# Loops written out and the gathers of the expert stage reordered in a spiking attention plus mixture-of-experts kernel

## The reference

```python
xn = layernorm(x)
Q, K, V = (spike(layer_norm(xn @ W.T + b, g, beta) - 1.0) for W in (Wq, Wk, Wv))  # 0 or 1
attn = (Dh - hamming(Q, K)) + log_pe_bias                # 16 heads of 16, no softmax
out = spike(attn * scale @ V - 0.5)
s = spike(layer_norm(out @ Wo.T + bo, go, betao) - 1.0)
r = rms_norm(xn) * ffn_scale
ids = argmin(dist2(r, centroids))                        # one expert of eight for each row
a, g = split(r @ up_w[ids])                              # 256 -> 2 x 512
y = (a * silu(g)) @ down_w[ids]                          # 512 -> 256
return x + s * silu(y + xn)
```

## Time and profile before

| | us |
|---|---|
| median of 3 runs (378.72 to 380.95) | 378.81 |
| the profiled execution | 379.37 |
| its span, first to last instruction | 377.6 |
| PE busy | 356.3 |
| DVE busy | 305.4 |
| ACT busy | 240.7 |
| POOL busy | 232.7 |

### The profile page before, as it was taken

One profiled execution on the slowest core, in us unless ns is written; L12 is line 12 of the kernel. 1 busy time (PEld: TensorE's weight loads), 2 busy tenths in 40 slices (PEclk: granted clock), 3 DMA queues, 4 the chain that ended last, 5 costly groups with the idle time before them and its releaser, 6 DMA issues.

```text
span 377.6 us, 9198 instructions
## 1 busy us (share of the span) xinstructions
PE 356.3 (94%) x2463; PEld 300.8 (80%) x2464; DVE 305.4 (81%) x783; ACT 240.7 (64%) x646; POOL 232.7 (62%) x295
## 2 busy tenths in 40 slices
PE   7999999999999999989977999999999999999992
PEld 4778888888877888867756888888888888888881
DVE  6989999998877798988648777778888777778874
ACT  5498899888956497865425656555555556555561
POOL 4877777877621169674664666666666666666642
PEclk9999999999999999999999999999999999999999
DMA  7596667555199634364131223222223233222000
GB/s 234 178 303 175 211 194 248 194 163 159 57 175 218 196 97 126 117 195 119 51 99 51 68 58 97 80 70 87 78 83 90 74 97 89 78 90 64 28 17 0
DMA packets 31921, 45.42 MB, mean 120 GB/s; under 512 B 4161, under 2 KB 25858, under 8 KB 31764
## 3 DMA queue, kind: packets, MB, share of 16 engines
q1 hardware_dynamic: 25248, 29.73, 27.0%
q0 software_dynamic: 6416, 15.26, 14.1%
q10 hardware_dynamic: 228, 0.10, 0.1%
HBM read 36.84 MB, written 15.63 MB: 139 GB/s over the span
## 4 chain that ended last, share of the span: by engine, by line
PE 73%; DVE 9%; POOL 4%; issue 4%; DMA 4%; ACT 2%; another core or an unknown queue 2%; ACTq 0%; POOLq 0%; DVEq 0%
PE bank L705 23%; PE bank L508 16%; PE bank L724 13%; PE bank L688 4%; PE bank L622 3%; PE bank L583 3%; DMA row_a<-rows_a,slot_id 3%; PE bank L677 3%; PE bank L487 2%; PE bank L586 2%; DVE up_lo L1309 1%; PE bank L522 1%; POOL pv L1515 1%; PE bank L526 1%
## 5 line engine op out<-in xcount | busy, mean ns | idle before, releaser
L1379 DVE TENSOR_TENSOR d_lo<-down_sb,d_hi 128x1024 fp32r<-128x1024 f32 x38 | 46.6, 1225 | 29.2 <-ACT d_hi L938 28.3
L1524 POOL DMA_INDIRECT row_a<-rows_a,slot_id x39 | 40.4, 1036 | 46.7 <-DVE e_o L1361 29.7
L938 ACT ACTIVATE d_hi<-down_sb 128x1024 fp32r x38 | 40.3, 1060 | 41.9 <-PE bank L724 20.0
L1577 POOL DMA_INDIRECT out_x<-e_o,slot_id x39 | 44.4, 1139 | 19.4 <-issue 14.4
L705 PE MATMUL bank<-up_hi,e_xh 128*128 x156 | 51.9, 414 | 0.5 <-ACT e_xh L909 0.5
L1530 POOL DMA_INDIRECT row_s<-rows_s,slot_id x39 | 41.0, 1051 | 16.0 <-issue 11.6
L705 PE MATMUL bank<-up_hi,e_xl 128*128 x156 | 48.5, 392 | 1.0 <-DVE e_xl L1320 1.0
L705 PE MATMUL bank<-up_lo,e_xh 128*128 x156 | 48.4, 391 | 0.0
L909 ACT ACTIVATE e_xh<-bank 128x256 fp32r<-128x256 f32 x39 | 15.0, 384 | 44.1 <-PE bank L677 20.7
L831 ACT ACTIVATE junk<-bank 128x256 bf16<-128x256 f32 x96 | 35.4, 378 | 2.9 <-PE bank L508 2.7
L508 PE MATMUL bank<-w_hi,x_hi 128*128 128x264 f32 (+1 forms) x128 | 35.5, 359 | 0.0
(11 more groups left out here) (243 smaller groups left out, 973.6 us busy)
## 6 DMA issues: line engine op xcount, KB each, us to landing
up_raw<-in_up_w SPq DMA_DIRECT2D x16, 512.0 KB, 4.3
rows_a<-xn SPq DMA_DIRECT2D x32, 129.0 KB, 2.4
rows_a<-in_x SPq DMA_DIRECT2D x8, 512.0 KB, 12.7
xs<-in_x SPq DMA_DIRECT2D x7, 512.0 KB, 3.8
down_sb<-in_down_w SPq DMA_DIRECT2D x5, 512.0 KB, 5.9
rows_s<-s_out SPq DMA_DIRECT2D x8, 256.0 KB, 2.8
down_sb<-in_down_w SPq DMA_DIRECT2D x6, 256.0 KB, 5.8
blk_tab<-in_blocks SPq DMA_DIRECT2D x1, 1024.0 KB, 6.9
```

The lines of the kernel that those rows point to most:

```text
L938: act.activation(d_hi[:, :, :], down_sb[:, bass.ds(e, 1), :, :].rearrange("p a c n -> p (a c) n"), ACT.Copy).then_inc(d_high, 1)
L1379: V.tensor_tensor(d_lo[:, :, :], down_sb[:, bass.ds(e, 1), :, :].rearrange("p a c n -> p (a c) n"), (d_hi if k < ST else d_end)[:, :, :].b ...
L1524: G.indirect_dma_start(row_a[s % 4][:, :], None, rows_a, bass.IndirectOffsetOnAxis(ap=slot_id[:, s:s + 1], axis=0), bounds_check=N - 1, oo ...
L1577: G.indirect_dma_start(out, bass.IndirectOffsetOnAxis(ap=slot_id[:, s:s + 1], axis=0), e_o[s % 4][:, :], None, bounds_check=N - 1, oob_is_ ...
```

## The change

In stage A, PE's loop becomes 24 written steps, k = 4 to 27; all counts and addresses in them are constants. In stage C, the loops of PE, ACT and DVE become 32 written steps each; the expert's number is still read into a register, but the counts in the waits are constants. With the loop, DVE's wait on `sent` comes back for the steps in which it was left out, since its condition `k - 2 >= 4` now sees the step's true number. POOL's loop in stage A stays.

On POOL the order of the indirect DMAs of stage C changes. Rows 0 to 3 and spikes 0 and 1 stay where they were. Then come, for s = 4 to 38: rows s, spikes s-2, output s-4; then spikes 37 and 38 and the outputs 35 to 38. The number of DMAs is the same.

```diff
@@ PE, stage A
             step_a(2, 0)
-            step_a(3, 0)
-            with pe.Fori(0, (NT - 8) // RA) as i:
-                for k in range(4, 4 + RA):
-                    step_a(k, i)
+            for k in range(3, NT - 4):
+                step_a(k, 0)
@@ PE, stage C (the same on ACT and DVE)
-            for k in range(4):
-                step_c(k, 0)
-            with pe.Fori(0, (ST - 4) // 4) as i:
-                for k in range(4, 8):
-                    step_c(k, i)
-            for k in range(ST // 4 * 4, ST + 2):
+            for k in range(ST + 2):
                 step_c(k, 0)
@@ POOL, stage C
             gather_s(0)
             gather_s(1)
-            gather_a(4)
-            gather_s(2)
-            gather_s(3)
 ...
             for s in range(4, ST):
-                if s > 4:
-                    gather_a(s)
+                gather_a(s)
+                gather_s(s - 2)
+                scatter(s - 4)
+            for s in range(ST - 2, ST):
                 gather_s(s)
-                scatter(s - 4)
             for s in range(ST - 4, ST):
                 scatter(s)
```

## The result

The changed kernel is faster by half a per cent: a median of 376.98 us (375.84 to 380.10) against 379.17 (376.83 to 381.60) for the kernel before, 20 executions of each, ratio 0.9951 with a 95% interval of 0.9929 to 0.9972. By the ratio that is 1.9 us, where 6.4 were forecast. It lies within the 1% that I had called "no change", and just outside the range.

A forecast was written before the change was run, and what follows sets the result against it. PE's own list was taken to set the pace, except in stage C's opening. Terms -6.1 (opening), -1.1 (stage A), 0, 0 and +0.8 (fetching) gave -6.4: span 377.6 to 371.2, time 372.4 us, range 368.0 to 376.6.

The forecast's parts named there:

- The opening: Start of stage C, tile 4 to tile 7: POOL's new order saves 6.1 us, or 2.5 if counts stay late.
- late counts: Opening of stage C: DVE and ACT start 3.15 and 2.1 us after the PE work they wait for, releaser "remote".
- unbroken run: POOL's 11 indirect DMAs without pause, 181.44 to 196.04 us, taken as the late counts' cause, by correlation only.
- Rival 1: Opening of stage C: late counts come back, only 2.8 us saved, 376.0 us; chance 0.17.
- Fetching the longer list: PE's instruction queue: 21 packets, 9 more, seven in stage C, holding up gathers; cost 0.8 us, bounds 0 and 4.8.
- the lag of 8.15: Steady stage C: us from a down product's end to a later gathered tile's transposes, against PE's own work of 8.02.
- The steady step of 5.0: Steady part of stage C: steps stay at 5.0 us; otherwise the lag or the fetching was mis-sized.
- Stage A: PE's loop written out saves 0.27 us of register work at six stalled steps: 1.1 us taken, bounds 0 and 1.6.
- Turns and waits: Loop turns in stages A and C, and DVE's added wait on `sent` and later spikes in C: zero cost or gain.
- rival 3: PE's loop turns in stages A and C cost one 1.0 us fetch each; 8 us more saved, 364.4; chance 0.02.
- Rival 4: PE's list can't be fetched in time; new packets stop PE or a gather, 4.5 us slower, 383.3; chance 0.05.
- Rival 2: Steady part of stage C goes dense, 4.85 us a step, 4.6 us more saved, 367.8; chance 0.10.

The follow-up runs named there:

- before, again: The kernel before, unchanged, profiled a second time; tile 4 to tile 7 took 21.19 us.
- PE's loop in stage C, again: Second run of the changed kernel with only PE's loop of stage C put back; ratio 0.9900 to the kernel before.
- fifth buffer, first set: Changed kernel with five gathered-row buffers instead of four, two output buffers, spikes s-3 and output s-5; first six executions: median 377.45 us, ratio 0.990 to before.
- the longer list on SP: Changed kernel with 2,400 more already-met waits at the end of SP's list; one execution, 375.33 us.

## Why the prediction was wrong

**The opening: right, and its parts.** Forecast -6.1, measured -5.7, with rows 5 no longer behind the spikes and tile 7's transposes 15.49 us after tile 4's ("15" in the prediction). By the prediction's own figures 2.5 of the 6.1 were waits for rows, and so 3.6 the late counts. The halves of the change tell the parts: with the loops written out and the old order it is 19.14, less 1.6 for the halved clock in that trace, 17.5. So 3.7 were late counts and 2.0 the order itself, by an estimate from one trace each. The size and the split came out; why the late counts went did not, as the next paragraph says.

**The cause of the late counts: refuted as stated.** I took POOL's unbroken run of indirect DMAs as the cause and called it a correlation. With the loops written out, the same order on POOL has the same run in the opening, and no late count. It can't be the sufficient cause. They also turned up in three other kernels, near the end of the kernel each time. What makes them isn't known from these runs. In the opening they stood in both profiles of the kernel with loops and the old order, and in none of the twelve others. That they are there in executions without a profile as well isn't shown: loops written out alone is 2.5 us slower by the median and 2.4 by its trace, but the granted clock, which differs between the two traces, is in these numbers too. So the forecast of 6.1 here was right by an argument that was not: its premise, the unbroken run, was wrong, and that the late counts went was luck. Rival 1, that they would come back, did not happen in the kernel after, in two profiles.

**Fetching the longer list: the step that failed.** The number of packets was nearly right (21 forecast, 22 found; seven more in stage C forecast, eight in its steady part alone), and the price was not: 0.8 us, where after is slower than POOL's order alone by 0.9951 - 0.9889 = 0.0062 of 379, 2.3 us, and writing out alone costs 4.2 in the steady part. The step went wrong at "near the low end, as only the packets of the transfer's own engine count". The upper bound of 4.8 was the better guide. A gather is done when its last piece is, so a packet in front of one piece delays the whole of it, and not a sixteenth: four gathers came 0.4 to 1.7 us late, and PE waited 0.5 to 1.5 us for each. I had written the lag of 8.15 against PE's own work of 8.02 myself: with nothing to spare, each such microsecond is PE's. So four of the eight packets cost, 0.58 + 0.60 + 0.50 + 1.52 = 3.2 us of waits, against 2.9 that the steady part grew by. How much of the time it is has a wide margin: PE's loop put back gained 0.9951 - 0.9886 = 0.0065, or 2.5 us, the first time, and 0.9932 - 0.9900, 1.2 us and not clear of noise, the second, when one packet met a gather in spite of the loop. The steady step of 5.0 that the prediction named as its test came out at 5.12 to 5.18 without a loop on PE.

By the Trainium skill, Runtime: NRT & Kernel Launch, Instruction fetch mechanics, the refill of a straight list runs ahead and is almost hidden. For PE's own waiting the traces agree: nine packets pass in the kernel with five buffers and PE never stops. For the kernel as a whole they disagree: the refill held up gathers, and cost 2.3 us by the medians above.

**Stage A: the other step that failed.** 1.1 us forecast, none found. The 0.34 us also after a stall did come, as this timeline of PE after shows:

```profile
80.24 0.27 PE L522 MATMUL bank<-ident,q_sp 128*128 128x128 bf16 x2 [0.21 <-DVE q_t L1137]
80.57 0.41 PE L487 MATMUL bank<-ident,xn 128*128 128x128 f32 x2
```

0.33 us with a wait in front, where it was 0.61. But PE had stopped because DVE was late; PE reaches the next wait earlier and waits longer. The waits of PE in front of L522 from 23.3 to 103.6 us, before and then after:

```profile
PEld bank L522 <- issue: 0.8, 3, 0.3
```

```profile
PEld bank L522 <- issue: 2.4, 7, 0.5
PE bank L522 <- DVE q_t L1137: 0.8, 3, 0.4
```

They grew by 1.6 us in front of the weight loads, which is the whole of what I had counted as saved. From tile 5 to tile 31 the stage takes 72.5 to 72.7 us in all 14 profiles. I had named this ("may give some of it back") and should have taken the lower bound. An engine's overhead after a wait for another engine was worth nothing in this stage, which the other engine paces.

**Turns and waits: right.** Writing out gave nothing at any turn, so rival 3 is refuted for these loops. The prediction says that the trace disagrees with the Trainium skill (Runtime: NRT & Kernel Launch, Instruction fetch mechanics) on taken branches, and that is too much. What stands there is for a branch to a block that is gone, and in the later passes of these loops hardly a packet was fetched. No run here shows what a turn costs where the block has to be fetched. DVE's wait on `sent` and the later spikes show up in no wait of the kernel after.

**What the order is worth by itself.** -5.8 in the opening of its trace, -4.2 by the median. Its steady part is 1.1 us longer than before's (5.07 to 5.03 a step), of which the repeat of the kernel before (5.06) gives back most; the rest isn't explained. So the whole reads: order about -4.2, writing out PE's stage C about +2.3, stage A, ACT and DVE 0, together the measured -1.9. Set beside the forecast's sum, by the traces: the opening -5.7 for -6.1, stage A 0 for -1.1, the steady part +2.9 for +0.8, and +0.2 at the end for 0; -2.6 for -6.4.

**A term that the sum lacks: the granted clock.** The prediction read 1.00 in its one trace and had no term for it. In five of the 14 profiles a stretch of 3.4 or 6.9 us in the middle of the work ran at the lower level: in the kernel with POOL's order alone in the first 15 us, and in the four others in stage C, where PE had stopped just before: 2.71 us (loops written out alone), 1.98 (before, again), 2.12 (PE's loop in stage C, again) and 3.83 (fifth buffer, first set), and the clock fell 0.3 to 1.4 us after it had taken up work. In the first profile of the kernel before, a stop of 2.05 us was not followed by it. The middle of the mean granted clocks is 0.992 in the 23 executions of the kernel before that ran beside the halves of the change, and 0.996 in the 20 of the kernel after, another group of runs. By these numbers, 0.004 of 377 us, or 3 us at half speed, a median execution before lost 1.5 us of work more to the clock, an estimate. So part of what the change gains may be the clock that stays up where PE no longer stops; no run separates it.

**The rivals.** Rival 4, "the list can't be fetched in time", had 0.05 and named the right cost, a packet that holds up a gather on the path; its size was between the forecast and the rival. Rival 2's dense steady part of 4.85 exists (4.87 and 4.88), but a fifth buffer is what gives it.

## What to carry to other kernels

Before a loop is written out on the engine that sets the pace, look for a transfer with no time to spare next to it: the longer list is fetched in 16 KB packets over the same DMA engines, and one that meets such a transfer can stop the engine that waits. Here they cost about 2.3 of the 4.2 us that the better order gained. The order in a queue that issues DMAs is worth what stands ahead of the one that is waited for, and can be costed from the timeline to a few tenths. Where an engine waits a little at every second step, try one more buffer before any saving of overhead: it gave 7.5 us here (2.0%) in four executions, and much less in five of six others, where late counts and a low clock were in the way. And read the granted clock of each stretch before two traces are set against each other: of an opening of 19.14 us, 1.6 were the clock.

## What the runs showed of the hardware that was not expected

- In the steady part of the kernel after, a 16 KB packet of instructions took 0.9 to 1.85 us. Four that started 1.0 to 1.8 us after the issue of a gather of 2056-byte rows had it used 0.5 to 1.8 us later than usual; a fifth in that range, at a gather of few rows, did nothing. In another trace, one at 3.05 made it 2.0. 14 packets of 8 KB instead of seven moved a step from 5.04 to 5.06 us only.
- Where such a packet falls is nearly the same from run to run: tiles 15, 22, 29 and 32 in both profiles of the kernel after, and with the longer list on SP. With PE's loop back in stage A those within 1.8 us of an issue fell at tiles 7, 14, 21, 28 and 31, and the gathers of 7, 14 and 31 were used after 4.78, 4.11 and 4.94 us.
- PE's granted clock fell to the lower level for 3.4 or 6.9 us after stops of 2.0 to 3.8 us in four profiles, and did not after one of 2.05 us in a fifth.
- A loop of 4 and one of 16 steps of PE were not fetched again in their later passes, but for a single packet in one of six profiles with a loop of 4.
- ACT and DVE waited up to 5.6 us for counts of PE on a semaphore, and the waits ended with nothing in the trace to release them: twice at nearly the same place in the kernel before, and near the end in three other kernels. No run shows why.
